# Sums over partitions by TensorE in the first stage, and the last attention's output projection from three bf16 parts of its weights

## What is computed

```
scale = jnp.maximum(jnp.mean(jnp.abs(w)), EPS)
q = _clamp_ste(_round_ste(w / scale))
...
amax = jnp.max(jnp.abs(wb), axis=(2, 4), keepdims=True)
safe = jnp.maximum(amax, W_EPS)
```

```
cat = jnp.concatenate([core, xout], axis=-1)
catq = _div_clamp_fp8(cat, proj_smooth)
return jnp.einsum('bsi,oi->bso', catq, wproj) * (proj_in_scale * proj_w_scale)
```

## Time and profile before

| | |
|---|---|
| median of 3 runs | 2537.11 us (2536.3 to 2540.7) |
| profiled execution | 2530.87 us, span 2529.1 us |
| mean granted TensorE clock | 0.895 of full speed |
| PE busy | 2090.0 us (83%) |
| DVE, ACT, POOL busy | 1620.9, 1076.7, 840.4 us |
| L0Attn, from its first scores | 38 to 371 us |
| L3Cross | 1647 to 2310 us |

### The profile page before, as it was taken

The page is one execution under the profiler, slowest core; times in us unless marked ns, Lnnn a source line. Parts: engine busy times, 40 slices in busy tenths (PEclk is TensorE's granted clock), DMA queues, the critical chain, the costliest instruction groups (busy, mean ns, idle before and its releaser), DMA issues. The chain is left out here.

```text
span 2529.1 us, 37639 instructions
## 1 busy us (share of the span) xinstructions
PE 2090.0 (83%) x13182; PEld 1499.2 (59%) x13257; DVE 1620.9 (64%) x4160; ACT 1076.7 (43%) x2451; POOL 840.4 (33%) x1360
## 2 busy tenths in 40 slices
PE   6887985699698458996559899959999999998991
PEld 4776772466365134554226576637888888785671
DVE  4664657545455855564657797858888888876333
ACT  1235632233243233442745755425555555553230
POOL 2225722211111211121000000046666766764444
PEclk9998996799798568997569999979999999998996
DMA  6013400000000030000000000031111111106553
GB/s 245 26 39 112 129 23 0 1 2 2 1 2 2 26 143 3 1 2 36 1 1 1 1 1 1 1 127 48 46 39 38 55 38 38 47 30 221 103 141 102
DMA packets 51130, 118.33 MB, mean 47 GB/s; under 512 B 6112, under 2 KB 23008, under 8 KB 48832
## 3 DMA queue, kind: packets, MB, share of 16 engines
q1 hardware_dynamic: 46096, 103.21, 11.8%
q0 software_dynamic: 4560, 12.46, 2.4%
q10 hardware_dynamic: 288, 0.26, 0.0%
HBM read 94.02 MB, written 19.79 MB: 45 GB/s over the span
## 5 line engine op out<-in xcount | busy, mean ns | idle before, releaser
L2769 POOL TENSOR_TENSOR K<-K 128x512 f32<-128x512 f32 x128 | 134.3, 1049 | 152.1 <-DVE K L2566 152.0
L2176 DVE TENSOR_TENSOR_SCAN W<-W,ps 128x512 f32<-128x512 f32 x128 | 155.6, 1217 | 40.3 <-issue 25.1
L1262 ACT ACTIVATE K<-ps 128x768 f32<-128x768 f32 (+1 forms) x128 | 110.5, 864 | 164.1 <-PE ps L1078 162.2
L2128 PEld LDWEIGHTS ps<-K 128*128 128x128 f32 x1024 | 136.7, 196 | 65.0 <-issue 51.0
L2709 ACT ACTIVATE K<-ps,K 128x256 f32<-128x256 f32 x128 | 60.6, 474 | 249.8 <-DVE K L2550 249.8
L2561 DVE TENSOR_SCALAR K<-ps,K 128x128 f32<-128x128 f32 x384 | 130.9, 403 | 26.9 <-POOL K L2786 26.6
L2128 PE MATMUL ps<-K 128*128 128x128 f32 x1024 | 139.3, 280 | 6.7 <-DVE W L2176 6.7
L1300 POOL CAST K<-K 128x8 bf16<-128x8 f32 x64 | 14.6, 229 | 365.8 <-issue 207.6
L2147 PE MATMUL ps<-W,C 128*128 128x512 f32 x256 | 132.2, 598 | 0.7 <-DVE W L2184 0.6
L2462 PE MATMUL ps<-K 128*128 128x256 f32 x512 | 131.8, 380 | 0.7 <-ACT K L2728 0.7
L2755 POOL TENSOR_SCALAR K<-K 128x1 f32<-128x1 f32 x16 | 3.6, 224 | 371.8 <-DVE K L2616 368.9
(11 more groups left out here) (515 smaller groups left out, 5784.8 us busy)
## 6 DMA issues: line engine op xcount, KB each, us to landing
W<-split_weights SPq DMA_DIRECT2D x32, 768.0 KB, 4.3
split_weights<-W SPq DMA_DIRECT2D x24, 384.0 KB, 2.5
W<-in_m SPq DMA_DIRECT2D x32, 256.0 KB, 4.8
results<-K SPq DMA_DIRECT2D x63, 128.0 KB, 2.4
W<-in_wproj SPq DMA_DIRECT2D x1, 4096.0 KB, 12.7
W<-in_m SPq DMA_DIRECT2D x32, 128.0 KB, 5.4
W<-split_weights SPq DMA_DIRECT2D x1, 3072.0 KB, 19.7
W<-in_Wq SPq DMA_DIRECT2D x1, 2048.0 KB, 11.5
```

What stands on the lines that cost most here:

```text
L1262: e.activation(to, made, ACT.Exp, scale=self.SCALE).then_inc(*self.up("exp"))
L2128: m = e.matmul(ps[1 + 2 * (n % 2)][:, b * 128:(b + 1) * 128], self.dtuT[h][:, i, b * 128:(b + 1) * 128], self.diag[s % 4][:, b * 128:(b + ...
L2176: e.tensor_tensor_scan(self.st[i % 3], self.a[i % 3], ps[1 + 2 * (i % 2)][:, :], 0.0, ALU.mult, ALU.add).then_inc(*sig.up("m scan"))
L2769: e.tensor_tensor(Pv, Pv, st[:, 4:6].unsqueeze(2).to_broadcast([128, 2, 256]), ALU.mult).then_inc(*sig.up("x scaled"))
```

## The change

**Sums over partitions.** The three `partition_all_reduce` sums go. In their place PE multiplies a 128x128 tile of ones (`self.ones`, set once by DVE) by the column of partial sums, so that each row of a PSUM column holds the total, and DVE reads it there. The maximum goes another way: PE transposes the 128x16 partial maxima, DVE takes the maximum along the row (16x128) and spreads it over 128 columns, PE transposes back. The context's scaling and rounding stand two steps later than before.

**Output projection.** `SplitWeights` has 40 blocks instead of 24 and starts a step earlier; the 16 new ones are `wproj`, and for these the scale falls away, so that ACT has two activations a block. L3Cross loads the 16 blocks of parts (6.3 MB) where it loaded `wproj` (4.2 MB); `normr` and one block move to K. `o8` becomes bf16. Each product with `wproj` becomes three bf16 products.

```diff
-    FIRST, N = 27, 24
+    FIRST, N = 26, 40
...
+        self.blocks += [("wproj", c * 512, None) for c in range(16)]
...
+        for i in range(1, 4):
+            part, _, _ = self.z(i)
+            t.wait_ge(sig["ternary part"], i)
+            t.e.matmul(bank[:, 32 + i:33 + i], self.ones, part, start=True, stop=True).then_inc(*sig.up("ternary sum"))
+            for _ in range(4 if i < 3 else 3):
+                yield
...
+        t.wait_ge(sig["ctx part"], 1)
+        t.wait_ge(sig["int8 kept"], 4)
+        t.e.transpose(bank[0:16, 256:384], self.f_rc, self.g.ident).then_inc(*sig.up("ctx part turned"))
+        yield
+        yield
+        t.wait_ge(sig["ctx max"], 1)
+        t.e.transpose(bank[:, 384:400], self.f_tmp[0:16, 0:128], C[0:16, 0:16]).then_inc(*sig.up("ctx max turned"))
...
-                e.partition_all_reduce(tot, part, 128, bass.bass_isa.ReduceOp.add).then_inc(*sig.up("ternary sum"))
...
-        e.partition_all_reduce(self.f_am, self.f_rc, 128, bass.bass_isa.ReduceOp.max).then_inc(*sig.up("ctx max"))
...
+            if i is None:
+                e.activation(self.part(n, 0), w, ACT.Copy).then_inc(*sig.up("split first"))
...
-                g.load(d, "wproj")
-                d.e.dma_start(g.normr, g.dram["normr"]).then_inc(*sig.up("x normr", 16))
+                g.parts_stored(d, 40)
+                for to, at in ((g.proj_parts, slice(24, 38)), (g.proj_last.unsqueeze(1), slice(38, 39)), (self.proj_end, slice(39, 40))):
+                    d.e.dma_start(to, g.parts[at].rearrange("b p n -> p b n")).then_inc(*sig.up("x proj parts", 16))
+                d.e.dma_start(self.normr, g.dram["normr"]).then_inc(*sig.up("x normr", 16))
...
-                        m = e.matmul(ps[7][:, a * 256:(a + 1) * 256], self.o8[n % 3][:, i * 256 + a * 128:i * 256 + (a + 1) * 128],
-                                     wproj[:, 2 * w + i, :], start=w == 0 and i == 0 and a == 0, stop=w == 15 and i == 1,
-                                     skip_group_check=True)
+                        for p in range(3):
+                            m = e.matmul(ps[7][:, a * 256:(a + 1) * 256], self.o8[n % 3][:, i * 256 + a * 128:i * 256 + (a + 1) * 128],
+                                         W[:, p * 512 + i * 256:p * 512 + (i + 1) * 256],
```

More of the change, by code:

```diff
@@ L308, in __init__ @@
         self.f_tmp, self.f_sum, self.f_am, self.f_rc = a.new(512), a.new(512), a.new(16), a.new(16)
-        self.small = a.new(12)
+        self.small, self.ones = a.new(12), a.new(128)
         g.tern = {}
@@ L388, in dve @@
                                            ALU.add).then_inc(v.own, 1))
+                v.step(e.memset(self.ones, 1.0).then_inc(v.own, 1))
                 v.wait_ge(v.own, v.n)
@@ L404, in dve @@
             v.wait_ge(sig["lane spread"], 1)
-            v.step(e.tensor_scalar(tot, tot if i else g.lane_total, 1.0 / 262144.0, eps, ALU.mult,
+            v.step(e.tensor_scalar(tot, self.bank[:, 32 + i:33 + i] if i else g.lane_total, 1.0 / 262144.0, eps, ALU.mult,
                                    ALU.max).then_inc(v.own, 1))
@@ L433, in dve @@
         yield
-        v.wait_ge(sig["ctx max"], 1)
-        v.step(e.tensor_scalar(am, am, 1e-6, None, ALU.max).then_inc(v.own, 1))
+        v.wait_ge(sig["ctx part turned"], 1)
+        v.step(e.tensor_reduce(self.small[0:16, 0:1], self.bank[0:16, 256:384], AX.X, ALU.max).then_inc(v.own, 1))
+        v.wait_ge(v.own, v.n)
+        e.tensor_copy(self.f_tmp[0:16, 0:128], self.small[0:16, 0:1].to_broadcast([16, 128])).then_inc(*sig.up("ctx max"))
+        yield
+        yield
+        v.wait_ge(sig["ctx max turned"], 1)
+        v.step(e.tensor_scalar(am, self.bank[:, 384:400], 1e-6, None, ALU.max).then_inc(v.own, 1))
         v.wait_ge(v.own, v.n)
@@ L516, in act @@
             a.wait_ge(sig[f"w split stored {n % 3}"], 16 * (n // 3))
-            a.step(e.activation(self.part(n, 0), w, ACT.Copy, scale=scale).then_inc(a.own, 1))
-            a.wait_ge(a.own, a.n)
-            e.activation(w, w, ACT.Copy, scale=scale).then_inc(*sig.up("split first"))
+            if i is None:
+                e.activation(self.part(n, 0), w, ACT.Copy).then_inc(*sig.up("split first"))
+            else:
+                scale = g.p("ins")[:, i:i + 1]
+                a.step(e.activation(self.part(n, 0), w, ACT.Copy, scale=scale).then_inc(a.own, 1))
+                a.wait_ge(a.own, a.n)
+                e.activation(w, w, ACT.Copy, scale=scale).then_inc(*sig.up("split first"))
         for n in self.at(s - 1):
@@ L2374, in __init__ @@
         self.rst, self.tok = a.ring(4, 40), a.ring(3, 512)
+        self.proj_end, self.normr = a.new(1, 768), a.new(256)
         self.fT = g.K[:, 2640:4688].rearrange("p (k n) -> p k n", k=2)
@@ L2417, in sp @@
         for e in range(14, 32):
+            if e == 31:
+                d.wait_ge(sig["x pair"], self.N // 2)
             g.load_expert(d, e)
@@ L2476, in pe @@
                 b, w = divmod(n, 16)
-                g.loaded(t, "wproj")
+                t.wait_ge(sig["x proj parts"], 48)
+                W = proj[w].bitcast(BF16)
                 t.wait_ge(sig["x o"], n + 1)
```

48 lines of the change are left out of this document (18 added, 30 removed).

## The result

The changed kernel takes 2495.88 us (median of four, 2487.62 to 2497.84) against 2536.7 us before: a ratio of 0.983, 95% interval 0.9805 to 0.9854. That is 40.8 us less, inside the range of 2487 to 2511 and 0.6 us from the 2496.5 that were predicted. That it came so close is luck: two terms of the sum were wrong in opposite directions, and each hid the other. The profiled execution (2487.62 us, span 2485.8) is the fastest of the four; a second profile of the same kernel has a span of 2491.0.

A forecast was written before the change was run, and what follows sets the result against it. PE's own work was taken to bound 1720 to 2280 us, and POOL's sums to stall the first attention. First stage -18.9 and last stage -21.7 make -40.6 us, from 2537.11 to 2496.5 us; range 2487 to 2511.

The forecast's parts named there:

- The four sums: First attention: PE's four steps made long by POOL sums lose their excess, -23.4 us.
- the +1.5 taken: First attention: +1.0 us for PE's five small products and transposes, +0.5 for the new waits.
- The maximum: First attention, context's maximum: step from 235.68 to 247.65 takes 11.97 us against 3.03, an excess of 8.94.
- the rounding of the context comes two steps later and costs what it did: First attention: the context's rounding moves two steps later at unchanged cost.
- The 16 blocks: End of the first stage: POOL falls behind with the 16 more split blocks, +3.0 us, bounds 0 and 14.
- A pair: Last cross attention, output projection: 1.31 us instead of 1.73, 0.42 less a pair, 64 pairs, -26.9 us.
- small waits: Last cross attention: PE's 6.9 us of small waits grow by half, +3.0 us, bounds 0 and 19.
- The first rival: Last stage: DVE's queue sets the step, only a third of the 26.9 is seen; 2511 us, chance 0.14.
- The sign that was to speak against me: Last stage's middle: idle PE of more than 15 us would show the forecast wrong.
- The last pairs: Last steps of the last stage: PE already waits for POOL, so the last three pairs give nothing, +1.2 us.
- the lead-in: Start of the last stage: q parts land later behind the projection's larger weights, +1.0 us, bounds 0 and 4.2.
- a wait for DMA of more than 5 us: Last stage's lead-in: L2505's first run waiting that long for DMA would show the forecast wrong.

The follow-up runs named there:

- two runs with the same stage: The kernel before with only the sums taken over by PE (2506.05 us), and the kernel before with only the context's maximum taken over by PE (2524.12 us).
- the sums alone: The kernel before with only the part of the diff in `WeightWork`: 2506.05 us against 2540.01, ratio 0.9864.
- the combined version: Changed kernel plus early context load, last six blocks' subtractions on DVE, and DVE's maximum ahead of row work in 21 steps: 2480.5 us, ratio 0.9774.
- the change of order: Changed kernel with DVE's maximum of the scores ahead of the row work in every step of the last cross attention: 2493.39 us, ratio 0.9832.
- two parts: Changed kernel with two instead of three bf16 parts in the output projection's products: 2493.23 us, ratio 0.9831.
- the q parts first: Changed kernel with the projection's parts loaded behind the first two groups' q parts and the second context load: 2494.24 us, ratio 0.9849.

## Why the prediction was right, and where it was not

**The four sums: right in kind, 6 us too small.** Sums and new waits together were to bring 21.9 us and brought 27.9. The three sums gave 13.7 us where the long steps 17, 21 and 25 had promised 14.5; the 0.8 between are the new waits and small PE operations in steps 18 and 22, less than the +1.5 taken. The maximum gave 14.3 us instead of 8.9. Two steps of the prediction failed there. I took the excess of the longest step, 38, for the whole price, where steps 36 and 39 to 41 had a share of 2.5. And "the rounding of the context comes two steps later and costs what it did" was assumed, not worked out: it costs 2.9 us less in its new place.

**The 16 blocks: right.** +3.1 us for the predicted +3.0, all of it at the end, and by the mechanism given: POOL takes the last norm 2.5 us after DVE has its moments.

**A pair: exact; how much of it is seen: wrong.** 1.31 us instead of 1.73, 0.42 a pair. But the term for "small waits", +3.0 with bounds of 0 and 19, was 11.2 (half of 6.9 us, as it was reasoned, would have been 3.5). I had measured the slack at the transposes L2453, behind POOL's scaling, in a short step; the tight row is another one, max, exponentials, ACT's copy of rows, next scores, in the steps in which DVE has row work. The first rival had named DVE's queue as the cause, and in ten steps it was right. Its row was there to be read: the 11 waits for L2742 above. The sign that was to speak against me, idle PE of more than 15 us in the middle of the stage, was missed only just: 14.1 us in 520.

**The last pairs and the lead-in.** The six pairs behind step 122 are worth 2.5 us and brought 0.9, so 1.6 were lost for the predicted 1.2. The lead-in was 0.85 us shorter in the profiles, where I had +1.0, but that compares two clocks. L2520 began 22.35 us after the stage's first load, 18.39 before, so 4.0 later for the predicted 4.2; DVE took up its result 0.7 us later, and the last L2537 ahead of the scores still began 0.7 later (34.20 us after the first load, 33.47 before). From there to the first scores the kernel before lost 1.6 us: these twelve products took 2.64 us there, at a granted clock of 0.50. In the two runs with the same stage they took 1.49, as in the changed kernel, and the lead-in was 36.26 us. Against these the changed kernel's 36.99 is +0.7, so the term was about right. The stage as a whole is the same in all three (663.2 to 663.5 us), because step 3 was slower in those two.

```profile
1680.49 2.64 PE L2522 MATMUL ps<-W,K 128*128 128x256 bf16 x12 [2.56 <-DVE K L2561]
```

The same products with the sums alone:

```profile
1653.37 1.49 PE L2529 MATMUL ps<-W,K 128*128 128x256 bf16 x12 [0.89 <-DVE K L2568]
```

I had set "a wait for DMA of more than 5 us" as a sign against me; it came, 5.20 us, and cost no more than that 0.7.

**The sum.** Measured stage by stage, -24.5 and -14.7 make -39.2, where -18.9 and -21.7 made -40.6. The first stage brought 5.6 us more than forecast and the last one 7.0 less, by mechanisms that have nothing to do with each other, so that the total says nothing for the forecast of either. The medians differ by 40.8 and 43.9 in two groups of runs. The 1.6 to 4.7 us between are within what stages with the same code vary by.

## What to carry over

A library instruction on POOL is dear by the pauses around it and what queues up behind them: follow the queue to the point where it has a gap again, not to the end of the longest step. When PE's work is cut in a stage where it has no idle time, look for the chains that are already within a few tenths of a microsecond of it, in the steps with the most side work, since every one of them turns the gain of all pairs since the last slack into waiting. Slack measured in one quiet step says nothing about these.

## What the runs showed of the hardware

**DVE's narrow operations wait for POOL.** The same int16 operation on 128x512 takes 0.30 us or 1.05 to 1.15. L2619 above ran from 1707.63 to 1708.68, beside POOL's scaling from 1707.49 to 1708.53, and ended 0.15 us after it. In the combined version the same work on rows fell between two POOL operations and took 0.29:

```profile
1707.70 1.15 POOL L2827 TENSOR_TENSOR C<-K 128x512 f32<-128x512 bf16 x1 [0.55 <-DVE K L2643]
1708.13 0.86 DVE L2679 TENSOR_SCALAR K<-K 128x512 bf16<-128x512 bf16 x1
...
1709.03 0.29 DVE L2681 TENSOR_SCALAR K<-K 128x512 int16<-128x512 int16 x1
```

The Trainium skill ("SBUF — State Buffer", "SBUF: two separate sides") says that GpSimd and certain DVE operations (those in a two-port mode, or with two inputs in SBUF) share a pair of ports as an exclusive lock, held for the whole instruction, so that the other is blocked and not slowed. The rows agree, with 0.14 to 0.15 us after POOL's end; which mode these operations run in they don't show. Whether this has a part in the 1.2 us that the change of order saved in step 11 is not shown: 5.64 us is what other steps of this kind (23, 55, 87) take in the changed kernel when PE doesn't wait at all.

**A pause of PE can cost more than its length.** In four steps of the last attention named above PE had waited 1.92 to 2.7 us at a granted clock of 1.00 (2.4 GHz), and the clock was 0.50 (1.2 GHz) for some 2 to 3 us within the step behind the wait: steps 12 and 96 with two parts, step 99 with the maximum first, step 3 with the q parts first. Each of these steps became 1.4 to 1.7 us longer. It does not follow each time: step 3 of the changed kernel has the same wait, 2.66 us, and kept 1.00. What decides is not in these rows. It means that one profile of a step with such a wait can be off by that much.

**Stages with the same code vary.** The first cross attention and the stage from the load of `e1` to that of `ctx` have the same code in all 14 kernels and took 702 to 711 us together in their profiles. The second of them was 247.5 us long at a granted clock of 0.89, 244.7 to 245.7 at 0.90, 242.8 to 244.2 at 0.91 and 241.5 at 0.92; the first took 459 to 469 us at 0.83 to 0.86. This alone is of the size of the differences between the four times of the changed kernel. What sets the clock there is open.
